# Regrouping copies laid over several steps, and a one-head attention stage written as a pipeline

## The reference, cut to what matters

```python
# block 3 (l0b): sixteen heads, no mask, the flat (tokens x channels) array is reshaped into heads
Q = (x @ Wq.T).reshape(H, b, s, dkh)
K = (x @ Wk.T).reshape(H, b, s, dkh)
V = (x @ Wv.T).reshape(H, b, s, dvh)
atten = softmax(einsum('hbqd,hbkd->hbqk', Q, K))
out = einsum('hbqk,hbkd->hbqd', atten, V).reshape(b, s, -1)
y = out + x;  y = (y - mean(y)) / sqrt(var(y) + EPS)

# block 7 (l1b): one causal head of width 128
K, Q, V = x @ Wk, x @ Wq, x @ Wv
wei = softmax(where(causal, (Q @ K.T) / sqrt(128), -inf))
wei @ V
```

## Time and profile before

| what | us |
|---|---|
| median of 3 runs | 4716.83 |
| lowest, highest | 4709.26, 4717.62 |
| profiled execution, its own time | 4705.67 |
| its span, first to last instruction | 4703.9 |
| busy in the span: PE, DVE, POOL, ACT | 3044.5, 2841.8, 2095.5, 1712.9 |
| sixteen-head grouped stage, first to last exponential | 548 |
| normalisation and one-head stage | 140.4 |

### The profile page before, as it was taken

How to read it: one execution, slowest core, us unless ns; L and a number is a source line. 1 busy time by engine, 2 the same in 40 slices (tenths; PEclk the granted TensorE clock), 3 DMA queues, 4 the chain that set the end, 5 groups by cost and what they waited for, 6 DMA issues and landing times. The chain is left out here.

```text
span 4703.9 us, 68286 instructions
## 1 busy us (share of the span) xinstructions
PE 3044.5 (65%) x23741; PEld 1871.1 (40%) x23741; DVE 2841.8 (60%) x6028; ACT 1712.9 (36%) x3024; POOL 2095.5 (45%) x2624
## 2 busy tenths in 40 slices
PE   5767266666294449559477746577655777566856
PEld 4667011111294238348233324333333333244534
DVE  4624567664435963342467659576577666486768
ACT  2412256554122224234245522355422355323511
POOL 6553311100344532322345368244495444396676
PEclk9778578786597769779699968699876899677867
DMA  5022222110131012002222100222000322000000
GB/s 151 38 79 69 65 72 68 52 51 1 52 94 53 0 50 63 14 16 62 63 61 69 43 0 1 62 76 62 23 0 8 79 70 65 1 0 1 1 0 18
DMA packets 218172, 206.30 MB, mean 44 GB/s; under 512 B 50439, under 2 KB 195015, under 8 KB 217080
## 3 DMA queue, kind: packets, MB, share of 16 engines
q1 hardware_dynamic: 205560, 176.85, 13.8%
q0 software_dynamic: 12288, 25.19, 1.8%
HBM read 103.55 MB, written 96.47 MB: 43 GB/s over the span
## 5 line engine op out<-in xcount | busy, mean ns | idle before, releaser
L918 DVE TENSOR_REDUCE l0b_negm<-l0b_ps_s 128x2 f32<-128x1024 f32 x256 | 303.0, 1220 | 164.4 <-PE l0b_ps_s L698 164.0
L786 ACT ACTIVATE l0b_E<-l0b_ps_t 128x1024 f32<-128x1024 f32 x256 | 261.8, 1023 | 233.1 <-PE l0b_ps_t L680 232.9
L918 DVE TENSOR_REDUCE l3a_negm<-l3a_ps_s 128x2 f32<-128x256 f32 (+3 forms) x256 | 199.1, 818 | 94.2 <-PE l3a_ps_s L704 94.0
L918 DVE TENSOR_REDUCE l2a_negm<-l2a_ps_s 128x2 f32<-128x256 f32 (+3 forms) x256 | 199.1, 819 | 89.9 <-PE l2a_ps_s L704 89.8
L918 DVE TENSOR_REDUCE l2b_negm<-l2b_ps_s 128x2 f32<-128x256 f32 (+3 forms) x256 | 199.2, 819 | 87.5 <-PE l2b_ps_s L704 87.0
L786 ACT ACTIVATE l3a_E<-l3a_ps_t 128x768 f32<-128x768 f32 (+1 forms) x192 | 169.1, 881 | 187.1 <-PE l3a_ps_t L680 186.8
L786 ACT ACTIVATE l2a_E<-l2a_ps_t 128x768 f32<-128x768 f32 (+1 forms) x192 | 169.2, 881 | 186.0 <-PE l2a_ps_t L680 185.6
L786 ACT ACTIVATE l2b_E<-l2b_ps_t 128x768 f32<-128x768 f32 (+1 forms) x192 | 169.2, 881 | 152.0 <-PE l2b_ps_t L680 151.9
L862 POOL TENSOR_SCALAR_AFFINE_SELECT l3a_E<-l3a_E 128x256 f32<-128x256 f32 x256 | 101.0, 406 | 220.5 <-ACT l3a_E L786 218.2
L862 POOL TENSOR_SCALAR_AFFINE_SELECT l2a_E<-l2a_E 128x256 f32<-128x256 f32 x256 | 101.0, 406 | 220.4 <-ACT l2a_E L786 218.0
L862 POOL TENSOR_SCALAR_AFFINE_SELECT l2b_E<-l2b_E 128x256 f32<-128x256 f32 x256 | 100.9, 408 | 217.7 <-ACT l2b_E L786 217.6
(11 more groups left out here) (1005 smaller groups left out, 9529.2 us busy)
## 6 DMA issues: line engine op xcount, KB each, us to landing
l0b_stack<-l0b_q_piece SPq DMA_DIRECT2D x48, 128.0 KB
l0b_stack<-l0b_k_piece SPq DMA_DIRECT2D x48, 128.0 KB
room_up<-l0b_stack SPq DMA_DIRECT2D x32, 192.0 KB, 3.2
room_down<-l0b_stack SPq DMA_DIRECT2D x32, 192.0 KB, 4.2
l2a_stack<-l2a_q_piece SPq DMA_DIRECT2D x48, 128.0 KB
l2a_stack<-l2a_k_piece SPq DMA_DIRECT2D x48, 128.0 KB
room_up<-l2a_stack SPq DMA_DIRECT2D x32, 192.0 KB, 4.1
room_down<-l2a_stack SPq DMA_DIRECT2D x32, 192.0 KB, 5.1
```

Of the source, the lines that this page charges most:

```text
L786: act.activation(probs(n % 3, c, 0)[:, 2 * p:2 * p + 2, :], ps_t[:, :, 0:width[c]], ACT.Exp, scale=scale).then_inc(probs_ready.sem, 1)
L918: e = dve.tensor_reduce(negm[:, qt, :, j], ps_s[n % 2][:, :, off:off + keys[qt]], AX.X, ALU.max, negate=True)
```

## The change

In the sixteen-head stage the sixteen copies of values on ACT (new line L813) are laid out four and four behind the exponentials of steps 13, 14, 15 and 16. The sixteen copies of `ungroup` on DVE (new L988) are laid out 3, 3, 1, 3, 3, 3 over steps 5 to 10; step 7, with one, is the one that also splits the maxima. The semaphores are raised by the last piece. The other heads stages are not grouped and keep their instructions.

The one-head stage is written anew. `norm_stage` ahead of it goes; the rows are normalised by `RowNorm` with one PSUM bank, two batches ahead. The product of the two projection matrices, times the scale, is formed once (wqk); q is projected with it and multiplied straight with XNT, so k, its projection and its copy go, as does xT and the scaling of the maxima. There is no loop instruction: the steps (batch, query tile) from -2 to 9 are written out. At a step TensorE makes the scores of this batch's tile, transposes the exponential of the same tile of the batch before, and multiplies the tile before that; projections of the next batch and the transposes of the one behind it stand between. qT, E, ET, y have two buffers, v and total three. The copy of v moves from DVE to ACT and the addition to X from DVE to GpSimd.

```diff
@@ -440,6 +440,7 @@
 K_ROWS = ((0, 16, 32), (8, 40), (24,))
 STACK = 48
 M_ROW = 48
+UNGROUP = (0, 3, 6, 7, 10, 13, 16)
 
 
 def heads_attention_stage(core, name, w, wo=None, bo=None, qk_bias=None, v_bias=None, rope=None, eps=0.0,
@@ -805,6 +806,14 @@
                         act.wait_ge(pieces_stored[a].sem, pieces_stored[a].after(PLACES * n))
                     act.activation(piece[a][0][:, :], ps_x[:, :], ACT.Copy).then_inc(first_piece.sem, 1)
 
+            def read_grouped_values(n, j):
+
+                for i in range(4):
+                    src = ps_x[32 * i:32 * i + 32, :].rearrange("p (t k j d) -> p k t j d", t=4, k=4, j=4)[:, :, :, j, :]
+                    a = act.activation(v1[n % 2][32 * j:32 * j + 32, :, i::4, 0:HD], src, ACT.Copy)
+                if j == 3:
+                    a.then_inc(spare_read.sem, 1)
+
             rows.normalise(act, 0)
             rows.read_transposes(act, 0)
             for T, b, g, l in steps():
@@ -833,15 +842,11 @@
                     in_spare(act, "v", n)
                     if n >= 2:
                         act.wait_ge(pv_ready.sem, pv_ready.upto((n - 1) * QUADS * NC))
-                    if grouped:
-                        for i in range(4):
-                            for j in range(4):
-                                src = ps_x[32 * i:32 * i + 32, :].rearrange("p (t k j d) -> p k t j d", t=4, k=4, j=4)[:, :, :, j, :]
-                                dst = v1[n % 2][32 * j:32 * j + 32, :, i::4, 0:HD]
-                                a = act.activation(dst, src, ACT.Copy)
-                    else:
-                        a = act.activation(v1[n % 2][:, :, :, 0:HD], ps_x[:, :].rearrange("p (t h d) -> p t h d", t=TB, d=HD), ACT.Copy)
-                    a.then_inc(spare_read.sem, 1)
+                    if not grouped:
+                        act.activation(v1[n % 2][:, :, :, 0:HD], ps_x[:, :].rearrange("p (t h d) -> p t h d", t=TB, d=HD),
+                                       ACT.Copy).then_inc(spare_read.sem, 1)
+                if grouped and 0 <= b + 1 < B and 0 <= g * L + l - (L + 5) < 4:
+                    read_grouped_values(b + 1, g * L + l - (L + 5))
 
         @block.gpsimd
         def _(pool):
@@ -970,17 +975,19 @@
                 dve.tensor_tensor(ao[:, :, c:c + 32].rearrange("p t (h d) -> p t h d", d=HD),
                                   pv[:, :, :, 0:HD], r, ALU.mult).then_inc(spare_read.sem, 1)
 
-            def ungroup(n):
-
-                dve.wait_ge(spare_read.sem, spare_read.upto(use["back", QUADS * n + 3] + 1))
-                if n >= 1:
-                    dve.wait_ge(out_read.sem, out_read.upto(n))
-                for i in range(4):
-                    for j in range(4):
-                        src = ao[:, :, :].rearrange("p k (t i d) -> p t k i d", t=4, i=4)[32 * j:32 * j + 32, :, :, i, :]
-                        dst = y[:, :, :].rearrange("p t (k j d) -> p t k j d", k=4, j=4)[32 * i:32 * i + 32, :, :, j, :]
-                        e = dve.tensor_copy(dst, src)
-                e.then_inc(out_ready.sem, 1)
+            def ungroup(n, part):
+
+                if part == 0:
+                    dve.wait_ge(spare_read.sem, spare_read.upto(use["back", QUADS * n + 3] + 1))
+                    if n >= 1:
+                        dve.wait_ge(out_read.sem, out_read.upto(n))
+                for k in range(UNGROUP[part], UNGROUP[part + 1]):
+                    i, j = k // 4, k % 4
+                    src = ao[:, :, :].rearrange("p k (t i d) -> p t k i d", t=4, i=4)[32 * j:32 * j + 32, :, :, i, :]
+                    dst = y[:, :, :].rearrange("p t (k j d) -> p t k j d", k=4, j=4)[32 * i:32 * i + 32, :, :, j, :]
+                    e = dve.tensor_copy(dst, src)
+                if part == len(UNGROUP) - 2:
+                    e.then_inc(out_ready.sem, 1)
 
             def add_output(n):
                 in_spare(dve, "out", n)
@@ -1028,8 +1035,8 @@
                     rows.shifts(dve, normed_at(T))
                     if normed_at(T) + 1 < B:
                         rows.statistics(dve, ch, normed_at(T) + 1)
-                if g == 0 and l == 5 and grouped and 0 <= b - 1 < B:
-                    ungroup(b - 1)
+                if grouped and 0 <= b - 1 < B and 0 <= g * L + l - 5 < len(UNGROUP) - 1:
+                    ungroup(b - 1, g * L + l - 5)
                 if g == 0 and l == L - 1 and 0 <= b < B:
                     split_maxima(2 * b + 1)
                 if g == 1 and l == 2 and projected and 0 <= b - 1 < B:
...
+        wqk = sb("wqk", [P, D])
+        qT = [sb(f"qT{u}", [P, S]) for u in range(2)]
+        v = [sb(f"v{u}", [P, TB, D]) for u in range(3)]
+        negm = sb("negm", [P, 2, TB])
+        E = [sb(f"E{u}", [P, TB, S]) for u in range(2)]
+        total = sb("total", [P, 3, TB])
+        rec = sb("rec", [P, 2, TB])
+        ET = [sb(f"ET{u}", [P, TB, S]) for u in range(2)]
+        y = [sb(f"y{u}", [P, TB, D]) for u in range(2)]
+        ps_q, ps_v, ps_o, ps_n = [psum(n, [P, S]) for n in ("ps_q", "ps_v", "ps_o", "ps_n")]
...
+        def steps():
+
+            for i in range(-2, B + 2):
+                for qt in range(TB):
+                    yield i, qt
...
+            def queries(b):
+                rows.wait_T(pe, b)
+                pe.wait_ge(qT_ready.sem, qT_ready.upto(b + 1))
+                pe.matmul(ps_q[:, :], wqk[:, :], core.XNT[:, b * S:(b + 1) * S], start=True, stop=True).then_inc(qT_in_psum.sem, 1)
...
+            def scores(b, qt):
+                m, n = b * TB + qt, P * (qt + 1)
+                if qt == 0:
+                    pe.wait_ge(qT_ready.sem, qT_ready.upto(b + 2))
+                if m >= 2:
+                    pe.wait_ge(probs_ready.sem, probs_ready.upto(m - 1))
...
+            def probs_back(b, qt):
+                m = b * TB + qt
+                pe.wait_ge(probs_ready.sem, probs_ready.upto(m + 1))
+                if m >= 2:
+                    pe.wait_ge(probsT_ready.sem, probsT_ready.upto(m - 1))
...
+            def attend(b, qt):
+                pe.wait_ge(probsT_ready.sem, probsT_ready.upto(b * TB + qt + 1))
+                if qt == 0:
+                    pe.wait_ge(v_ready.sem, v_ready.upto(b + 1))
+                    if b >= 1:
+                        pe.wait_ge(out_read.sem, out_read.upto(b))
...
+            pe.matmul(ps_q[:, 0:D], w[:, 0:D], w[:, D:2 * D], start=True, stop=True).then_inc(qT_in_psum.sem, 1)
+            for i, qt in steps():
+                if 0 <= i < B:
+                    scores(i, qt)
+                if 0 <= i + 1 < B and qt == 1:
+                    queries(i + 1)
+                if 0 <= i + 1 < B and qt == 2:
+                    values(i + 1)
+                if 0 <= i + 2 < B and qt == 2:
+                    rows.transposes(pe, i + 2)
+                if 0 <= i - 1 < B:
+                    probs_back(i - 1, qt)
+                m = (i - 1) * TB + qt - 1
+                if 0 <= m < B * TB:
+                    attend(m // TB, m % TB)
...
+            act.wait_ge(qT_in_psum.sem, qT_in_psum.upto(1))
+            act.activation(wqk[:, :], ps_q[:, 0:D], ACT.Copy, scale=scale).then_inc(qT_ready.sem, 1)
+            for i, qt in steps():
+                if 0 <= i < B:
+                    exponentials(i, qt)
+                if 0 <= i + 2 < B and qt == 1:
+                    rows.normalise(act, i + 2)
+                if 0 <= i + 1 < B and qt == 2:
+                    act.wait_ge(qT_in_psum.sem, qT_in_psum.upto(i + 3))
+                    if i >= 1:
+                        act.wait_ge(scores_ready.sem, scores_ready.upto(i * TB))
+                    act.activation(qT[(i + 1) % 2][:, :], ps_q[:, :], ACT.Copy).then_inc(qT_ready.sem, 1)
+                if 0 <= i + 1 < B and qt == 3:
+                    act.wait_ge(v_in_psum.sem, v_in_psum.upto(i + 2))
+                    if i >= 2:
+                        act.wait_ge(out_ready.sem, out_ready.upto(i - 1))
+                    act.activation(v[(i + 1) % 3][:, :, :], ps_v[:, :].rearrange("p (t d) -> p t d", t=TB), ACT.Copy).then_inc(v_ready.sem, 1)
+                if 0 <= i + 2 < B and qt == 3:
+                    rows.read_transposes(act, i + 2)
+
+        @block.gpsimd
+        def _(pool):
+            for i in range(-2, B + 2):
+                if 0 <= i + 2 < B:
+                    rows.roots(pool, i + 2)
+                if 0 <= i - 2 < B:
+                    b = i - 2
+                    pool.wait_ge(out_read.sem, out_read.upto(b + 1))
+                    x = core.X[:, b * TB:(b + 1) * TB, :]
+                    pool.tensor_tensor(x, x, y[b % 2][:, :, :], ALU.add).then_inc(out_added.sem, 1)
...
+            rows.statistics(dve, ch, 0)
+            for i, qt in steps():
+                if 0 <= i < B:
+                    maximum(i, qt)
+                if 0 <= i + 2 < B and qt == 0:
+                    rows.shifts(dve, i + 2)
+                if 0 <= i - 1 < B:
+                    read_probs(i - 1, qt)
+                if 0 <= i - 2 < B and qt == 0:
```

(7 more changed lines are left out.)

145 lines of the change are left out of this document (57 added, 88 removed).

## The result

The changed kernel takes 4631.47 us (median of 4 runs, 4627.72 to 4641.52); the kernel before, run beside it, 4713.05 (4706.18 to 4717.62). The ratio is 0.9831 with a 95% interval of 0.9817 to 0.9845, a saving of 81.6 us where 69.6 were forecast. The profiled execution fell from 4705.67 to 4627.72 us, its span by 77.9 us to 4626.0.

What follows compares the result with a forecast made beforehand. Stages run one after another, so only the two touched count: ACT and DVE bound the sixteen-head steps, waits between phases the one-head turns. 19.6 + 13.2 + 36.8 = 69.6 us off the median 4716.83 gives 4647, range 4624 to 4670.

Steps and rivals of the forecast that it cites:

- Part 1: Sixteen-head stage, values' copies on ACT spread over four steps: exponentials 13 to 17 save 2.8 us x 7 batches, 19.6 us.
- Part 3: One-head stage rewritten: 103.6 us against 140.4, at 10.1 us per full batch; 36.8 us saved.
- Part 2: Sixteen-head stage, ungrouping copies on DVE over steps 5 to 10: 12 us in five batches, 1.2 in batch 6, together 13.2.
- rival (c): Both stages: TensorE at half rate throughout, one-head stage 33 us longer, 12.2 lost in sixteen-head; time 4729, chance 0.03.
- The walk along VectorE's queue: Sixteen-head stage, batch 2's DVE times followed from maximum 5: exponential 11 comes 11.3 us after exponential 8, against 13.66.
- rival d: Sixteen-head stage: exponentials 8 to 11 take batch 0's 6.56 us in batches 1 to 5, 35.5 us; time 4624, chance 0.15.
- rival a: Sixteen-head stage: spread ungrouping copies stay blocked by GpSimd, so the 13.2 us become -5; time 4665, chance 0.12.
- (b): One-head stage: pipeline stays at 13.06 us per batch, only the start is saved, 16.1 us; time 4668, chance 0.10.
- The marks that I had set: Signs of being right in both stages' profile, among them a 10.1 us one-head turn and granted clock above 0.95.
- One sign of being wrong: Stages outside the two changed ones: any of them longer by more than 2 us would count against the forecast.

Runs made afterwards that it cites:

- late split: Changed kernel, with GpSimd's splitting held back until the exponential of step 14 is done: 4623.84 us, ratio 0.978; changed kernel beside it 4654.23.
- with two buffers: Changed kernel, with two buffers for the grouped outputs and the ungrouping copies put off to steps 13 to 16, four in each: 4609.28 us, ratio 0.9753.
- with the reductions: Changed kernel, with the sixteen ungrouping copies written as tensor_reduce maxima over an axis of length one: 4641.1 us, ratio 0.981; changed kernel beside it 4654.23.
- with all three: Changed kernel, with values' copies over six steps, two grouped-output buffers with ungrouping at steps 13 to 16, and one-head shifts last: 4601.96 us, ratio 0.9718.

## Why the prediction was right, point by point

**The time.** 4647 was forecast from a median of 4716.83, with 4624 to 4670 as the range; it came to 4631.47, inside. That it came so near is in part luck: three terms were off, and they cancelled in part. Part 1 gave 10 us less than booked, Part 3 12 more, the last batch 8 where nothing was booked, and Part 2 2 more.

**Part 1 (19.6 us) was too large.** Steps 13 to 17 gave 16.6, and 7.1 were lost again in steps 17 to 32: 9.5 net, below my lower end of 14. Two steps of the working failed. The first is the length of a full step: 2.22 us and not 2.09. I took the 0.08 by which two instructions overlap from places where ACT had nothing queued; between an exponential and the copies behind it there is 0.03 of gap instead. The second weighs more: I wrote that the three slow steps behind the long one "were under 2.09 too" and left the clock there. The stretch at half rate did not go away, it moved behind the copies. The earlier trace rows had both sorts of the stretch from 17 to 21, 9.14 us at 0.56 and 6.69 at 1.00, and I had priced the slow sort only in the rival (c). It should have stood in the sum: six batches of seven now run there at half rate for a part of it, where two did, and that costs 5.3 us.

**Part 2 (13.2 us) was right in size**, and in what bounds these steps, but not in where the gain came from. Steps 8 to 11 fell from a mean of 13.66 us to 11.07 in batches 1 to 5 (11.3 forecast), 13.0 us in all, and by 1.84 in batch 6 (1.2 forecast). The walk along VectorE's queue came nearer than both simple rules, "the batch becomes like batch 0" (rival d) and "the collisions eat the gain" (rival a). In the batch that was walked, though, the copies and the small operations met GpSimd in other places than the walk had them, and the batch took 10.52 us and not 11.3. Summed over batches 1 to 5, the first ten copies, which stay in these steps, took 24.9 us before and 28.4 after (25.9 in the second trace of the changed kernel); the last six took 17.0 before, and after the change they stand behind maxima 9 and 10 and take 6.6 us, hardly stretched. So the gain is six copies moved out of the steps together with their collisions (17.0), less 3.5 us that the others collide more, less 0.5 of the small operations. Rival (a) was right that the copies left in these steps would collide as much as before or more; it missed the six that no longer do.

The reason that I gave for the walk, that VectorE has 10.3 us of its own work between maximum 5 and maximum 9 "whatever the collisions", is wrong. Where nothing collides (late split, batch 1) that work takes 8.1 us, from 683.21 to 691.28. The steps take 6.8 us with the copies in a form that does not collide, 6.2 with GpSimd silent and 4.8 with the copies elsewhere, so some 4 to 5 us of the 11 are collisions.

**The last batch (not booked) gave 7.8 us.** It ran at a clock of 0.86 and not 0.66. In each of the fourteen traces the batch begins at full clock, steps of 1.51 us and so 3.02 for two; from where the clock falls to half, two steps take 4.13 us. The length of the batch is set by when that happens, counted from its first exponential: after 15.9 us in the kernel before and with the new one-head stage alone (61.6 us long), 21.5 to 21.8 with two buffers, with the reductions and with all three (60.2 to 60.5), 26.0 with the ungrouping alone (58.7), and 38.9 to 39.1 in the seven other traces that have both regroupings (53.8), the changed kernel's two among them. With the values alone (59.8) it was down from 13.8 to 17.2 and again from 27.5 on. What decides when it falls stays open: no rule that I tried covers these times.

**Part 3 (36.8 us) was too small by 11.6.** The term that failed is 7 x 10.1 = 70.7 us for the turns behind the first batch. They took 8.4, four times 9.89, 7.7 and 6.3, together 62.0. A full turn was well sized (9.89). But the pipeline projects one batch ahead and transposes two ahead, so the turn before the last has no transposes of normalised rows and the last has no projections either (2.2 and 3.6 us less than a full turn); I had multiplied where I should have listed the turns. The first batch took 6.3 and not 8, the start 10.8 and not 11.5, and the tail 9.2 and not 9.5. The content of a full turn was also not as forecast: TensorE is busy 8.62 us and not 9.42, since I had carried over the matmuls' lengths from the loop: the scores of 512 columns took 745 ns there and take 594 here, the transposes of exponentials 303 and 274, at equal counts per batch (why they are shorter is not shown; the clock was 0.96 and is 1.00). And it waits 1.0 us for a division that stands behind an answer of GpSimd, where I had allowed 0.7 for statistics ahead of a maximum. Moving the shifts took this wait away: 8.88 us.

**The rivals.** (b), a turn of 13.06, fell. (c), half rate in both stages, fell for l1b (clock 1.00) and its price for l0b's steps 17 to 21 came true in part, 5.3 us of 12.2. The measured 4631.47 is nearer to (d)'s 4624 than to the forecast's 4647, but not by (d)'s mechanism: steps 8 to 11 were nowhere near batch 0's length in batches 1 to 5. The marks that I had set: steps 8 to 11 at 10.5 to 11.9 us in batches 1 to 5 (11 to 11.5 said), ACT's longest wait at step 11 is 4.48 us in batch 2 and 5.09 in batch 3 (under 5 said), one table load (as said), steps 13 to 17 at 8.7 to 9.04 (8.4 said), TensorE at 87% of a turn (over 90 said). One sign of being wrong did show: two stages that the change leaves alone, l0a and l3b, are 3.4 and 2.6 us longer. Over the traces here the same two stages lie between 158.6 and 162.5 and between 202.6 and 205.9 us with unchanged code, so that mark was too tight to mean anything.

## What to carry to other kernels

When small copies on VectorE lie beside GpSimd's instructions, look at their single lengths: if one form of instruction has lengths from 0.2 to 1.2 us that end with GpSimd's, look for another form (a reduction over an axis of one, 13 us here on top of the spreading), or another place (30 us by a later start of GpSimd's chain, 37 by a second buffer that let the copies wait), before being content with spreading them. Of a pipeline list the turns one by one, the first and last without the work that runs ahead, before multiplying. A saving ahead of steps that TensorE bounds has to be booked together with the clock of those steps, and a wait for a slow engine's answer belongs behind everything that others wait for in the same queue.

## What was not expected of the hardware

- The same 222 matmuls of the last batch take 53.8 us at a mean granted clock of 0.86 or up to 61.6 at 0.66, by when the clock falls to half for most of the rest: 13.8 to 39.1 us into the batch. Edits that move at most the ungrouping's sixteen copies within this batch decide it, and the point was the same in both profiled executions of the changed kernel (38.9 and 39.0) and of the sixteen-head code before (15.9). The cause is open.
- In batch 2, sixteen copies over four steps were followed by a stretch at 0.60 of the clock, over six steps by one at 1.00, with TensorE busy 6.57 us of 9.04 and 6.15 of 8.16 in the steps ahead. Other batches and kernels break the pattern, so what the clock follows there is open.
- A copy of 32 partitions by 128 elements from SBUF to SBUF took 0.22 us alone and up to 1.23 beside GpSimd, the same bytes as a reduction 0.28 in either case. GpSimd's instructions, 0.61 to 0.69 and 1.15 to 1.24 us, hardly noticed the copies.
- Two series of runs differ by more than small gains: the changed kernel had medians of 4631.47 and 4654.23 us, with the kernel before at 4713.05 and 4729.5.
